# The band mask of an attention kernel: added to the scores by TensorE instead of multiplied into the probabilities by VectorE

## What is computed

```python
def _blocked_mask(seq_len):
    i = jnp.arange(seq_len)[:, None]
    j = jnp.arange(seq_len)[None, :]
    return (j <= i) & (j >= i - WINDOW)                  # WINDOW = 16
...
scores = jnp.einsum('bhqd,bhkd->bhqk', q * scale, k)
blocked = _blocked_mask(s)
scores = jnp.where(blocked[None, None, :, :], -jnp.inf, scores)
attn = jax.nn.softmax(scores, axis=-1)
ctx = jnp.einsum('bhqk,bhkd->bhqd', attn, v)
```

## Time and profile before

| | |
|---|---|
| median of 3 runs | 2005.11 us (2003.32 to 2005.72) |
| the profiled execution: its own time | 2009.24 us |
| the profiled execution: its span | 2007.5 us |
| ScalarE busy | 1912.3 us (95%) |
| TensorE busy with matmuls / weight loads | 1823.5 us (91%) / 751.8 us (37%) |
| VectorE busy | 887.3 us (44%) |
| GpSimd busy | 867.0 us (43%) |
| granted clock of TensorE, mean | 0.99 |

### The profile page before, as it was taken

The page is one execution under the profiler, slowest core; times in us unless marked ns, Lnnn a source line. Parts: engine busy times, 40 slices in busy tenths (PEclk is TensorE's granted clock), DMA queues, the critical chain, the costliest instruction groups (busy, mean ns, idle before and its releaser), DMA issues.

```text
span 2007.5 us, 100828 instructions
## 1 busy us (share of the span) xinstructions
PE 1823.5 (91%) x46728; PEld 751.8 (37%) x46728; DVE 887.3 (44%) x1527; ACT 1912.3 (95%) x2099; POOL 867.0 (43%) x738
## 2 busy tenths in 40 slices
PE   7799999999999999999999999999998888888895
PEld 4333344343434434343343434344342323223232
DVE  6223343645465364546536454554633313242332
ACT  4599999999999999999999999999999999999993
POOL 2000005628083562908347191744719253464500
PEclk9799999999999999999999999999999999999998
DMA  4410111101231110111221111111022111000111
GB/s 132 130 33 28 50 33 43 54 17 40 78 83 43 43 50 21 48 36 48 66 66 50 40 51 37 49 49 33 18 78 56 33 32 33 19 26 27 28 36 34
DMA packets 93454, 93.81 MB, mean 47 GB/s; under 512 B 17562, under 2 KB 84570, under 8 KB 93026
## 3 DMA queue, kind: packets, MB, share of 16 engines
q1 hardware_dynamic: 92772, 87.05, 14.8%
q10 hardware_dynamic: 256, 0.26, 0.1%
HBM read 52.56 MB, written 25.72 MB: 39 GB/s over the span
## 4 chain that ended last, share of the span: by engine, by line
ACT 60%; issue 28%; PE 8%; DVE 2%; DMA 1%; SPq 1%; POOL 0%; DVEq 0%
ACT probs L1274 60%; PE outs L1341 2%; PE ps_qk L493 2%; PE scores L1322 1%; DVE probs L927 1%; PE ps_v L510 1%; SPq L162 0%; PE spare L1424 0%; DVE s_parts L1007 0%; DVE t_under L1111 0%; DMA inverse<-row_inverse 0%; PE ps_turn L463 0%; DVE s_qk_f L995 0%; DVE s_qk_f L998 0%; DMA xin<-in_x 0%
## 5 line engine op out<-in xcount | busy, mean ns | idle before, releaser
L1274 ACT ACTIVATE probs<-scores 128x1024 f32<-128x1024 f32 x2048 | 1882.8, 1107 | 27.6 <-PE scores L1322 26.8
L1341 PE MATMUL outs<-probs,vs 64*32 64x512 f32 x16384 | 1077.2, 590 | 1.5 <-DVE probs L927 0.8
L1322 PE MATMUL scores<-qs,ks 49*32 49x512 f16 x16384 | 840.5, 383 | 141.8 <-ACT probs L1274 129.4
L1322 PEld LDWEIGHTS scores<-qs,ks 49*32 49x32 f16 x16384 | 232.9, 89 | 1065.2 <-ACT probs L1274 1030.1
L1341 PEld LDWEIGHTS outs<-probs,vs 64*32 64x32 f32 x16384 | 302.1, 106 | 32.0 <-issue 6.0
L927 DVE TENSOR_TENSOR probs<-probs,allowed 128x320 f32<-128x320 f32 (+2 forms) x280 | 193.5, 700 | 245.9 <-ACT probs L1274 245.4
L872 POOL TENSOR_SCALAR t_over<-t_over 128x512 f32<-128x512 f32 x140 | 211.8, 1513 | 12.3
L871 POOL TENSOR_TENSOR t_over<-t_over,t_square 128x512 f32<-128x512 f32 x140 | 184.7, 1320 | 11.7
L813 POOL TENSOR_TENSOR s_var_eps<-s_mean_var,eps 128x4 f32<-128x4 f32 x12 | 2.4, 201 | 407.8 <-DVE s_mean_var L968 407.8
L827 POOL TENSOR_TENSOR s_squares<-s_qk_f 128x512 bf16<-128x512 f32 x48 | 56.2, 1180 | 242.7 <-DVE s_qk_f L998 242.0
L1380 PE MATMUL spare<-s_xt,w_qkv 64*32 64x256 f32 x3072 | 121.7, 375 | 0.1
(11 more groups left out here) (136 smaller groups left out, 1213.9 us busy)
## 6 DMA issues: line engine op xcount, KB each, us to landing
qs<-q_parts SPq DMA_DIRECT2D x192, 64.0 KB
ks<-k_parts SPq DMA_DIRECT2D x192, 64.0 KB
inverse<-row_inverse SPq DMA_DIRECT2D x32, 256.0 KB
ctx_in<-raw SPq DMA_DIRECT2D x248, 32.0 KB, 2.0
out<-s_pre SPq DMA_DIRECT2D x15, 512.0 KB, 5.0
s_xin<-in_x SPq DMA_DIRECT2D x12, 512.0 KB, 4.7
q_parts<-s_parts SPq DMA_DIRECT2D x24, 256.0 KB, 2.2
k_parts<-s_parts SPq DMA_DIRECT2D x24, 256.0 KB, 4.1
```

What stands on the lines that cost most here:

```text
L1274: act.activation(probs[:, u % RING, 2 * slot:2 * slot + 2].rearrange("p c q -> p (c q)"), scores[:, 2 * slot:2 * slot + 2].rearrange("p c ...
L1322: last = pe.matmul(scores[cols, 2 * slot + e], ks[rows, group, keys], qs[rows, group], start=True, stop=True)
L1341: last = pe.matmul(outs[32 * c:32 * c + 32, side], vs[keys, at:at + 2 * HD], probs[keys, u % RING, c], start=(i == 0), stop=(i == KBLOCKS ...
```

## The change

The exponential of a masked score has to be zero. The kernel after the change adds a large negative number to such a score while it is still in PSUM. For that each half of the partitions of a new float16 tile `barred` holds (allowed - 1) x 65504, and `pick` holds 4096 on its diagonal. In a masked unit each slot of scores is followed by 8 more matmuls of 64 rows by 32 columns over at most 80 columns, with `pick` as weights and `barred` as what streams, accumulated on the scores. `mask(u)`, its semaphore, the wait of `weigh` for it and the tables for that are gone. GpSimd makes the two tiles in the first stage.

```diff
+BARRED = 65504.0
+BARRED_BY = 4096.0
...
+                pool.tensor_scalar(keep["barred"][side * HALF_P:(side + 1) * HALF_P], half, 1.0, BARRED, ALU.subtract,
+                                   ALU.mult).then_inc(keep["barred_ready"], 1)
+                pool.tensor_scalar(keep["pick"][side * HALF_P:(side + 1) * HALF_P],
+                                   ident[side * HALF_P:(side + 1) * HALF_P, side * HALF_P:(side + 1) * HALF_P],
+                                   BARRED_BY, 1.0, ALU.mult, ALU.mult).then_inc(keep["barred_ready"], 1)
...
         @block.vector
         def _(dve):
-            def mask(u):
-                _, qc, _, _, kb = unit(u)
-                lo, cols, at = masked_columns(qc, kb)
-                dve.wait_ge(exped, 2 * u + 2)
-                tiles = probs[:, u % RING, :, lo:lo + cols]
-                keep_row = keep["allowed"][:, at:at + cols].unsqueeze(1).to_broadcast([P, HG, cols])
-                dve.tensor_tensor(tiles, tiles, keep_row, ALU.mult).then_inc(masked, 1)
...
                 for r in range(STEP):
-                    seen = step * STEP + r - 2
-                    if seen >= 0 and MASKS_BEFORE[seen + 1] > MASKS_BEFORE[seen]:
-                        mask(seen)
...
+                if u == 0 and slot == 0:
+                    pe.wait_ge(keep["barred_ready"], 4)
...
                         last = pe.matmul(scores[cols, 2 * slot + e], ks[rows, group, keys], qs[rows, group],
-                                         start=True, stop=True)
+                                         start=True, stop=barred is None)
+                if barred is not None:
+                    lo, count_of, at = barred
+                    for quarter in range(4):
+                        part = quarter % 2
+                        cols = slice(quarter * 32, quarter * 32 + 32)
+                        for e in range(2):
+                            rows = slice(e * HALF_P, (e + 1) * HALF_P)
+                            last = pe.matmul(scores[cols, 2 * slot + e, lo:lo + count_of],
+                                             keep["pick"][rows, part * 32:part * 32 + 32],
+                                             keep["barred"][rows, at:at + count_of], start=False, stop=True)
                 last.then_inc(scored, 1)
...
                 pe.wait_ge(exped, 2 * u + 2)
-                if MASKS_BEFORE[u + 1] > MASKS_BEFORE[u]:
-                    pe.wait_ge(masked, MASKS_BEFORE[u + 1])
```

More of the change, by code:

```diff
@@ L120, in bass_preln_layer @@
             "allowed": sb("allowed", [P, FAST_BAND]),
+            "barred": sb("barred", [P, FAST_BAND], F16),
+            "pick": sb("pick", [P, HALF_P], F16),
+            "barred_ready": sem("barred_ready"),
             "flag": sb("flag", [1, 1], I32),
@@ L599, in stream @@
         exped = sem("exped")
-        masked = sem("masked")
         summed = sem("summed")
@@ L670, in unit @@
             return b, qc, hg, i, key_order(qc)[i]
[L672 to L679, removed]
         def weighed_at(position):
@@ L1310, in score @@
                 _, qc, hg, i, kb = unit(u)
+                barred = masked_columns(qc, kb)
                 if slot == 0 and i == 0:
                     pe.wait_ge(lay["qs_in"][hg], loads_until(u // STEP))
+                if u == 0 and slot == 0:
+                    pe.wait_ge(keep["barred_ready"], 4)
                 if u:
```

## The result

| | before | after |
|---|---|---|
| median on the same chip (4 runs each) | 2005.41 us (2003.32 to 2007.34) | 2022.74 us (2020.88 to 2025.01) |
| ratio, 95% interval | | 1.0087 (1.0074 to 1.01) |
| the profiled execution | 2009.24 us | 2020.92 us |

The change costs 17 us, 0.9%. The two profiled executions differ by only 11.7 us, since that of before lay over its median and that of after under it.

What follows compares the result with a forecast made beforehand. ScalarE was taken to set the time, with TensorE close behind. On the median of 2005.1 us, -5 for VectorE's gaps, +6.5 for short groups and +5 for late instructions gave 2011 us, range 1998 to 2029.

Steps and rivals of the forecast that it cites:

- rival B: TensorE's short groups: weight loads set the pace, 0.09 us a group or more; 2024 us, up to 2032; chance 0.22.
- ScalarE sets the time, and TensorE keeps up with little to spare: Steady state: ScalarE needs 1.836 us a unit, TensorE 1.75 with a piece, so 0.09 us to spare.
- I take all six gaps as gone: -5 us: ScalarE's six gaps behind VectorE in steps 7, 10 and 11, 4.75 us together, vanish with the masks.
- So the price lies between 0.034 and 0.09, and I take 0.063: TensorE's cost in us per short group; over 184 masked units with a piece it adds 6.5 us.
- Masked units with a piece take 1.87 us: Sign in the profile after: such units slow to 1.87 us, masked units without a piece stay at 1.836.
- 0.28 from slot to next group: Sign on TensorE: 0.28 us from the start of a slot with its short group to the next group.
- Together +5 us, between 0 and 12: Late TensorE instructions: 2.2 us for 115 more units with 128, and 3 us for 57 units with 160.
- A (short groups as good as free): Short groups on TensorE cost 0.034 to 0.044 us each, within both margins; 2002 us, 1999 to 2007; chance 0.32.
- C, the rule of about 25 ns between starts: Each of a group's eight short matmuls takes its own turn on TensorE, 0.2 us a group; 2071 us; chance 0.04.
- VectorE busy 170 us less (I said 190): Sign in the profile after: VectorE is busy some 190 us less without its 280 masks.
- no gap with `s_qk_f` behind it in steps 7, 10 and 11: Sign on ScalarE: none of its gaps there still has that wait behind it after the change.
- "issue" waits risen at r = 47 to 54: Sign on TensorE: weight loads wait more there with no engine waited for, as instructions come late.

Runs made afterwards that it cites:

- e1: The kernel before with the mask left out and nothing in its place: 2007.28 us, ratio 0.9994 against before.
- e12: The kernel after, but VectorE masks the 57 masked units with a piece of the values' projection, TensorE the 223 others: 2009.89 us, 1.0014 against before.
- e3: The kernel after, but VectorE masks in the second half of the projecting steps and TensorE everywhere else: 2008.88 us, 1.0001 against before.
- e6: The kernel after with the mask added by four matmuls of 64 x 64 per slot instead of eight of 64 x 32: 2115.23 us, 1.0536 against before.
- e9: The kernel before with the values piece as 16 matmuls on 64 x 64 tiles instead of 32 on 64 x 32: 2016.11 us, 1.0041 against before.
- e2: The kernel after with short matmuls over 8 columns instead of up to 80, same number of instructions: 2027.52 us, 1.0095 against before.
- e7: The kernel after with each short group issued twice at r = 15 to 23 of the twelve projecting steps: 2060.24 us, 1.0272 against before.
- e10: The kernel before with 32 idle semaphore increments on TensorE's queue at r = 47 and 51 to 54 of the projecting steps: 2300.25 us, 1.1451 against before.

## Why the prediction came out as it did

The forecast was 2011 us and slower; measured were 2022.7, inside the range and outside the forecast's own 2004 to 2018. That it lies in the range is partly luck: the part above 2018 stood there for rival B, whose mechanism was not at work. The sum foresaw +6.5 us and 17.3 were measured. The sign rested on the right mechanism, late instructions, but all three terms had the wrong size, and their errors went opposite ways.

*"ScalarE sets the time, and TensorE keeps up with little to spare".* Right. The steady pace stayed at 0.918 us, and the exponentials have not become longer.

*"I take all six gaps as gone: -5 us".* The mechanism was right, the gaps are gone in after and in e1, and with them 5.8 us of B in the one profile. As a term of the time it was too large: e1, which takes away nothing else, gains 0 to 3.4 us. The six gaps were most likely a matter of one execution.

*"So the price lies between 0.034 and 0.09, and I take 0.063".* Measured: 0.04, near the lower bound, and then the term is zero, since 1.75 + 2 x 0.04 = 1.83 fits. The step that failed is the choice of the middle. The sum itself pointed at the threshold, 0.045 a group, and the row that was nearest, slots of 512 columns at 0.22, gave 0.034. The uncovered loads behind the group, for which I added half of what the transpositions showed, cost 0.006. E shows it best: 35 masked units with pieces, and 2.9 us lost against 3.3 before. "Masked units with a piece take 1.87 us" was wrong, they take 1.834; "0.28 from slot to next group" was 0.26 to 0.27.

*"Together +5 us, between 0 and 12" for instructions that come late.* This was the decisive term, and it was three to four times too small. C alone lost 19.1 us. The reason the term gave is the one that the runs found, and the units it named (r = 47 and 51 to 54) are the ones that e12 singles out. What went wrong is the price: I took 3 us for the 57 units with 160 instructions because none was in the trace, and bounded them by 10. Now 13 to 15 us come from them, some 0.25 us each. The gaps of before, 0.019 us per unit with 128, were a count just under a threshold, and no basis for what lies over it. The records would have given a better sum. From where TensorE enters a piece of 256 to where the transfer of the next one starts, before has a median of 0.78 us, and in one piece out of ten over 1.40; from there to where TensorE goes on in a stop, 2.4 us. A piece lasts 256 / 128 x 1.83 = 3.7 us at 128 instructions a unit, which leaves 1.3 us for the first part, so that some are late; at 160 it lasts 2.9 us and leaves 0.5, so that most are. That is an estimate from these figures, made after the result, and it has the edge where the runs found it.

*The rivals.* A (short groups as good as free) is right on its own step, and its time is wrong for the other term. B's 2024 is the nearest to what was measured, yet by another mechanism: e3 shows no weight load that sets the pace. C, the rule of about 25 ns between starts (the Trainium skill, TensorE: Matmul & The Clock Gate, "Wait — 56ns, not 53.3ns?"), would have made 0.2 us a group: eight starts fell within 0.04 us, so it does not hold between different tiles.

*"What would show it".* VectorE busy 170 us less (I said 190); no gap with `s_qk_f` behind it in steps 7, 10 and 11; "issue" waits risen at r = 47 to 54, yes, and as far as r = 58, behind the dense units and not only in them.

## What to carry to other kernels

Count the instructions of a stretch as well as its work: here TensorE kept its pace, but for a few stops, up to 128 instructions per 1.83 us and lost it at 160, although the array would have done them in time. The sign in a profile is an "issue" wait in the midst of a group with no engine behind it, and if before shows a few, more instructions at that place are dear at once. A term that was worked out from gaps of one execution needs a second look at how often these gaps come: VectorE's gaps stood in the profile of before, and taking the masks away altogether (e1) won at most 3.4 us of the median.

## What the runs showed of the hardware that was not expected

- A change of the tile's shape on TensorE costs about 0.12 us each way: 0.35 instead of 0.22 us from a slot to a 64 x 64 group, 0.16 instead of 0.04 behind it (e6), and 0.33 instead of 0.22 (e9). From 49 x 32 to 64 x 32 it costs nothing (0.22). The Trainium skill (TensorEngine Tiling (Array Packing), "Key Properties") says that changing the tiling mode drains the engine; the traces agree, and put this price on it.
- Eight matmuls of 64 rows by 32 columns over 80 columns, side by side on eight tiles, take 0.04 us with their weight loads, and with 8 columns the kernel is no faster (e2). A second such group on the same tiles right behind the first adds about 0.1 us (e7).
- An increment of a semaphore on TensorE's queue takes about 0.13 us (e10).
- TensorE stops at the edge of a piece of 256 instructions, for up to 1.6 us at a time after the change (2.8 us once in e1, at 1934 us), and goes on 1.2 to 1.6 us behind the end of the transfer. At up to 128 instructions per 1.83 us the stops beside C are 7 (before); with 57 units at 160 they are 31.
